# Input statistics handed over from the first stage, their normalisation moved to ScalarE, square roots in place of Newton steps, a transposed shared expert, and weights loaded behind the activations

## The chip, the cores and the metric

The kernel runs on one core of one Trainium2 chip. The metric is the device time of one execution in microseconds (us), the median of several. Before the change three runs gave 4096.03 us (4090.68 to 4097.14).

## What is computed

A small vision tower over 128 images. Tokenising gives 169 tokens of 128 values for each image; two layers follow, each of an attention and a feed-forward part, all with a residual and a layer norm in front. In short:

```
h = tok(x)                                    # 5 shifted contexts, norm, 8x8 patches -> (128, 169, 128)
h = h + neuron_attention(norm(h))             # 256 neurons, softmax(scale / (dist + 0.1))
h = h + fp8_linear(norm(h), weight)           # 128x128, scaled by the largest |norm(h)| of all tokens
h = h + softmax(n n^T / sqrt(512)) n          # n = norm(h), over the 169 tokens of an image
h = h + shared_experts(n) + routed(n)         # n = norm(h); 2 shared, 64 routed, 6 of them for a token
```

The routed part: a router gives logits (with a bias), the six best experts of each of the 21632 tokens get a gate, each expert takes at most 4056 tokens, and computes silu(n wg) * (n wu) times its down matrix.

## The kernel before

**Front stage** (`front`, some 850 us). All images' tokens stand in SBUF. It makes `h` up to the neuron attention (`h1`), in 43 groups of four token positions, keeps mean and variance of each token in `mv1`, from which it finds the largest normalised value, and stores `h1` to DRAM (`h1d`).

**Middle stage** (first part of `back`). Two chains are braided by `braid` in numbered steps. A 'b' part runs for a pair of images in each of 64 steps: the fp8 linear and the attention over tokens. An 'r' part runs for a group of 512 rows of the result, 43 groups, in two of every three steps: norm, router, shared experts, ranks. `place_of` says in which step a group comes, `LATE` how many steps behind the pairs the groups begin. A part's number in the list is its lag: at lag 1 it works for the pair or group of the step before. Steps therefore come in threes: one without 'r' work (here called P, pair only), and two with it, Q (the one after P) and R (the one after Q). The lists in each engine's block give the order of the parts on that engine, and an engine takes them strictly in that order.

In a step VectorE (DVE) runs: `ffn_out` (adds the fp8 product to `h1`, statistics of the sum), `stats_q` (statistics of the next pair's `h1`), `choose` (logits, best experts), `silu_gate`, `attn_out`, `place`, `roots` (reciprocals of the roots that ScalarE makes), `norm_x`, `quant` (normalise `h1` and round it to fp8 values), `silu_up`, `denominator` (its last instruction completes a row, L1569), `norm` (statistics of the group, `rsqrt` by three Newton steps, the normalised row) and `shared_out`. TensorE (PE) runs: `count`, `shared_up`, `turn_x`, `scores`, `turn_q`, `ffn`, `turn_h`, `shared_down`, `mix`, `turn_r`, `route`. ScalarE (ACT) runs: `tanh`, `roots`, `probs`, `copy_x`, `expo`, `copy_q`, `copy_h`, `copy_x4`.

GpSimd (POOL) writes the finished rows (token, gates and its number) to the expert row buffer `xed` in DRAM, one indirect DMA for 128 rows and one choice: 24 for a group, 1014 in all (L991). A memset on a one-column tile behind each (L996) paces them. `norm` of group g waits until the 24 of group g-4 have landed, since `xr` has four buffers.

**Expert stage** (second part of `back`). `tables_late` turns the counts into lists of row blocks. SyncE (SP) loads four blocks of 128 rows at a time into `xin` (`load_rows`, here the same memory as `xr`), PE, ACT and DVE compute the experts, and POOL writes each block's results to `ytk` by an indirect DMA (`spread`, L1003, 1080 of them). After the first eight loads SP writes 64 blocks of `xed` with a neutral row (L1093). Near the end `add_up` sums the six results of each token.

**At the head of `back`** SP loads all weights of the second layer (L1028 to L1032), then the first `h1` (L1018); DVE waits for all of it and halves `wdt` (L1391), and PE and ACT wait too.

What sets the steps' numbers:

```python
    LATE = 7
    CUT = place_of(GSTEPS[0][1], LATE) + 1
```

and the wait behind which the loads of rows stand:

```python
            sp.wait_ge(n["tab_ready"], 2)
            scattered_up_to(GR)
```

Of the kernel before, what the change touches and what calls it, by code (L numbers as in the profile page):

```python
# [127 lines left out]
def braid(eng, begin, end, late, parts, r_first, r_stop):  # L128
# [8 lines left out]
    def do(i, u):  # L137
        third, m = (u - late) % 3, (u - late) // 3
        c = 2 * m + (third == 2)
        for kind, lag, fn in parts:  # L140
            if kind == 'b':
                g = period * i + (u - lag)
                if not isinstance(g, int) or 0 <= g < nb + (lag == 0 and fn.__name__ == "roots"):
                    fn(g, (u - lag) % 2, 3 * i + (u - lag) // 2)
# [19 lines left out]
def build(nc, io):  # L164
# [11 lines left out]
    with ExitStack() as ctx:  # L176
# [3 lines left out]
        def sem(name):  # L180
# [14 lines left out]
        fscale = sb("fscale", [128, 4])  # L195

        front(nc, io, sb, bank, wide, dict(
            ident=ident, identb=identb, ones=ones, onesb=onesb, before=before, beforeb=beforeb,
            eps_ln=eps_ln, tenth=tenth, wq=wq, fscale=fscale), h1d, gbd, ytk)
        back(nc, io, sb, sem, bank, wide, dict(  # L200
            ident=ident, identb=identb, ones=ones, onesb=onesb, before=before, beforeb=beforeb,
            wq=wq, fscale=fscale, eps_ln=eps_ln), h1d, h3d, h4d, xed, ytk, out)


def front(nc, io, sb0, bank, wide, c, h1d, gbd, ytk):
# [7 lines left out]
    with ExitStack() as ctx:  # L213
        def sb(name, shape, dt=F32):
            return sb0(name, shape, dt, ctx)
# [56 lines left out]
        zeros = sb("zeros", [128, 768])  # L272
# [21 lines left out]
        with nc.Block() as block:  # L294
# [24 lines left out]
            def _(g):  # L319
# [7 lines left out]
                g.memset(zeros[:, :], 0.0).then_inc(s_zero, 1)  # L327
                g.wait_ge(s_const, 7)
# [156 lines left out]
        s_amall = sem("s_amall")  # L485

# [4 lines left out]
        with nc.Block() as block:  # L491
            @block.sync
            def _(sp):
# [19 lines left out]
                sp.wait_ge(s_zero, 1)  # L513
# [32 lines left out]
            def _(pe):  # L546
# [49 lines left out]
                pipeline(pe, 0, GA, [(2, turn), (4, turn_probs), (2, cross), (4, mix), (0, conv)])  # L596

# [58 lines left out]
            def _(v):  # L656
# [102 lines left out]
                link(v.reciprocal(hmin[:, :], hstd[:, :]))  # L759
                link(v.tensor_tensor(hmax[:, :], hmax[:, :], hmin[:, :], ALU.mult))  # L760
# [13 lines left out]


# [13 lines left out]
def rsqrt(v, var, eps, out, xe, half, done, base):  # L789

    v.tensor_scalar(xe, var, eps, None, ALU.add).then_inc(done, 1)
    v.wait_ge(done, base + 1)
    v.tensor_scalar(half.bitcast(I32), xe.bitcast(I32), 1, None, ALU.logical_shift_right).then_inc(done, 1)
    v.wait_ge(done, base + 2)
    v.tensor_scalar(out.bitcast(I32), half.bitcast(I32), -1.0, float(0x5F3759DF), ALU.mult, ALU.add).then_inc(done, 1)
    for k in range(3):
        v.wait_ge(done, base + 3 + 3 * k)  # L800
        v.tensor_tensor(half, out, out, ALU.mult).then_inc(done, 1)
        v.wait_ge(done, base + 4 + 3 * k)
# [1005 lines left out]
```

## Time and profile before

| | before |
|---|---|
| median of 3 runs | 4096.03 us (4090.68 to 4097.14) |
| the profiled execution, its own time | 4103.54 us |
| its span | 4101.7 us |
| mean granted TensorE clock | 0.678 |
| PE busy | 2888.1 us (70%) |
| DVE busy | 2655.3 us (65%) |
| ACT busy | 1512.4 us (37%) |
| POOL busy | 2720.8 us (66%) |

The span counts from the first to the last instruction. Busy shares are means over stages with different limits; the sections below read single stages. In the trace's rows a time in brackets is how long the engine had stood idle before the instruction, and the name behind the arrow what ended it. SPq is SyncE issuing a transfer.

### The profile page before, as it was taken

The numbers are of one execution on the slowest core, as the hardware profiler recorded it, in microseconds if no ns is written. First come the engines' busy times: TensorE is split into PE (matmuls) and PEld (weight loads), VectorE is DVE, ScalarE is ACT, GpSimd is POOL, SyncE is SP. The second block draws the span as 40 slices with busy tenths as digits, with TensorE's granted clock in tenths as the row PEclk, the third lists the DMA queues.
The fourth block names the chain that finished last, engine by engine and source line by source line (L and its number), as shares of the span: only waits on it lengthen the run. The fifth ranks groups of instructions, "written<-read, shape, count | busy, mean of one in ns | idle before, by whom it ended". The sixth has DMA issues, their size and how long they took to land. (4 is left out here: it accounts for less than half of the span.)

```text
span 4101.7 us, 75982 instructions
## 1 busy us (share of the span) xinstructions
PE 2888.1 (70%) x14869; PEld 2249.8 (55%) x14870; DVE 2655.3 (65%) x10164; ACT 1512.4 (37%) x3699; POOL 2720.8 (66%) x4427
## 2 busy tenths in 40 slices
PE   2988888727777777777767752687777777767770
PEld 2767777614544445454544531576676666666660
DVE  4588888846888888888778761344444444466664
ACT  2566666613232323323223211333433344333330
POOL 1355555400687777777757886588888888887881
PEclk7699999855555555555555556677878888877675
DMA  3555555321233333333323224544444444489867
GB/s 158 173 194 189 196 185 186 138 79 29 93 120 106 118 104 116 102 105 93 97 69 93 91 79 117 153 139 140 142 141 138 139 142 134 134 261 290 263 175 256
DMA packets 427082, 582.16 MB, mean 142 GB/s; under 512 B 64858, under 2 KB 345594, under 8 KB 415444
## 3 DMA queue, kind: packets, MB, share of 16 engines
q1 hardware_dynamic: 343668, 418.11, 33.7%
q0 software_dynamic: 83232, 162.29, 11.7%
q14 instruction: 149, 1.22, 0.1%
q8 instruction: 33, 0.54, 0.1%
HBM read 299.55 MB, written 306.56 MB: 148 GB/s over the span
## 5 line engine op out<-in xcount | busy, mean ns | idle before, releaser
L991 POOL DMA_INDIRECT xed<-xr,idxs x1014 | 1002.4, 989 | 528.0 <-POOL pace L996 188.9
L1003 POOL DMA_INDIRECT ytk<-yo,idxy x1080 | 1078.7, 999 | 297.5 <-POOL pace L1008 207.5
L1242 PE MATMUL wide<-wdt,hT 64*128 x2160 | 374.3, 323 | 360.4 <-DVE hT L1720 359.6
L1702 DVE TENSOR_TENSOR idxy<-xr 128x1 int32<-128x1 f32 x1080 | 148.2, 163 | 643.7 <-DMA ytk<-yo,idxy 640.9
L1242 PEld LDWEIGHTS wide<-wdt,hT 64*128 64x128 f32 x2160 | 314.3, 221 | 416.3 <-issue 413.7
L1378 ACT ACTIVATE yo<-wide,gd 128x128 f32<-128x128 f32 x1080 | 307.8, 368 | 633.7 <-PE wide L1242 615.9
L1224 PE MATMUL bank<-wgu,xeT 128*128 x2160 | 388.7, 340 | 0.0
L1224 PEld LDWEIGHTS bank<-wgu,xeT 128*128 128x128 f32 x2160 | 369.6, 258 | 1.5
L537 POOL TENSOR_TENSOR lnr<-rr,scb 128x1024 f32<-128x1024 f32 (+1 forms) x43 | 125.0, 2907 | 354.3 <-ACT rr L631 354.3
L1151 PE MATMUL wide<-xn,e 128*128 128x128 f32 (+3 forms) x1024 | 324.1, 449 | 0.0
L526 POOL TENSOR_TENSOR weff<-w,gam 128x640 f32<-128x640 f32 x169 | 260.7, 1571 | 86.3 <-POOLq L294 77.0
L1214 PE MATMUL bank<-ident,xr 128*128 128x128 f32 x1080 | 225.0, 347 | 100.8 <-DMA xr<-xed 100.8
L554 PE MATMUL bank<-weff,xs 128*128 128x128 f32 x1690 | 258.1, 306 | 14.7 <-DMA gbx<-gbd 14.7
L1151 PEld LDWEIGHTS wide<-xn,e 128*128 128x128 f32 (+3 forms) x1024 | 182.0, 234 | 124.4 <-issue 123.0
L554 PEld LDWEIGHTS bank<-weff,xs 128*128 128x128 f32 x1690 | 230.2, 214 | 32.8 <-DMA gbx<-gbd 15.7
L1363 ACT ACTIVATE xeT<-bank 128x512 f32<-128x512 f32 x270 | 163.2, 604 | 210.4 <-PE bank L1214 210.2
L1214 PEld LDWEIGHTS bank<-ident,xr 128*128 128x128 f32 x1080 | 179.1, 184 | 107.5 <-issue 101.3
L1140 PE MATMUL bank<-xnT 128*128 128x169 f32 (+1 forms) x512 | 202.3, 523 | 37.4 <-ACT xnT L1307 37.4
L1233 PE MATMUL wide<-ident,hh 128*64 128x128 f32 x1080 | 220.3, 341 | 0.0
L1130 PE MATMUL bank<-ident,xn 128*128 128x128 f32 (+1 forms) x256 | 87.5, 394 | 151.8 <-DVE xn L1451 151.8
L592 PE MATMUL bank<-v,eT 128*128 128x128 f32 x676 | 128.9, 369 | 82.9 <-issue 74.0
L1720 DVE COPY hT<-wide 64x512 f32<-64x512 f32 x270 | 182.1, 674 | 6.9 <-PE wide L1233 6.9
(312 smaller groups left out, 5918.6 us busy)
## 6 DMA issues: line engine op xcount, KB each, us to landing
xr<-xed SPq DMA_DIRECT2D x1080, 113.0 KB
ytk<-zeros SPq DMA_DIRECT2D x42, 1536.0 KB, 9.4
yg<-ytk SPq DMA_DIRECT2D x42, 1536.0 KB
xs<-in_xcol SPq DMA_DIRECT2D x42, 1280.0 KB
ytk<-yo,idxy POOLq DMA_INDIRECT x1080
xed<-xr,idxs POOLq DMA_INDIRECT x1014
H<-in_ximg SPq DMA_DIRECT2D x4, 2704.0 KB, 18.1
h1d<-H SPq DMA_DIRECT2D x42, 256.0 KB, 2.0
```

Source lines behind the costliest of these rows:

```text
L526: ins = p.tensor_tensor(weff[:, slot, j, :, :], w5[:, :, :], gam[:, bass.ds(TG * g + j, 1), :].rearrange("p o c -> p (o c)").unsqueeze(2). ...
L554: pe.matmul(dst, xs[:, slot, j, k, :], weff[:, slot, j, k, :], start=(k == 0), stop=False)
L991: p.indirect_dma_start(xed[:, :], bass.IndirectOffsetOnAxis(ap=idxs[:, slot, j, k:k + 1], axis=0), xr[:, slot, j, :], None, bounds_check=Z ...
L1003: p.indirect_dma_start(ytk[:, :], bass.IndirectOffsetOnAxis(ap=idxy[:, slot, j:j + 1], axis=0), yo[:, slot, j, :], None, bounds_check=128 ...
L1140: last = pe.matmul(dst, xnT[:, i, 128 * h:128 * h + m], xnT[:, i, 0:T], start=True, stop=True)
L1151: last = pe.matmul(pP[0:m, 256 * i + D * h:256 * i + D * h + D], e[0:m2, i, 128 * h:128 * h + m], xn[0:m2, slot, 2 * i + h2_, :], start=(h ...
L1214: last = pe.transpose(eT_[slot % 2][:, j * 128:(j + 1) * 128], xin[:, slot, j, 0:D], ident[:, :])
L1224: last = pe.matmul(eG[slot % 2][:, j * 128:(j + 1) * 128], xeT[:, slot % 2, j, :], wgu[:, bass.ds(e, 1), :].rearrange("p o f -> p (o f)"), ...
L1233: last = pe.transpose(eH[slot % 2][0:F, j * 128:(j + 1) * 128], hh[:, slot % 2, j, :], ident[:, :])
L1242: last = pe.matmul(eO[slot % 2][:, j * D:(j + 1) * D], hT[:, slot % 2, j, :], wdt[:, bass.ds(e, 1), :].rearrange("p o f -> p (o f)"), star ...
L1378: last = a.activation(yo[:, slot, j, :], eO[slot % 2][:, j * D:(j + 1) * D], ACT.Copy, scale=gd[:, slot, j:j + 1])
L1720: v.tensor_copy(hT[:, slot % 2, :, :].rearrange("p j d -> p (j d)"), eH[slot % 2][0:F, :])\
```

## The change

- The front stage transposes `mv1`'s means and reciprocal deviations on PE into a new table `mur` (scale and bias for each token of each pair, with the fp8 scale in it).
- `stats_q` is gone. ACT gets `norm_q` at the head of each step: a copy of eight values from `mur`, then four activations that write the scaled, normalised `xq`. `quant` on DVE keeps the clamp and the rounding.
- `roots` becomes `root_x` (root of the pair's variance, lag 1) and `root_r` (root of the group's, lag 0); `rsqrt` is gone. DVE takes the group's statistics at the head of the step (`stats_r`).
- The shared experts' gate and up products have the weights as the stationary operand and the 512 rows as the moving one: one product in place of four, with a transposed result. `turn_h` and `copy_h` are gone.
- The halves in `wdt` and `sdt` move into the gates and into `shared_out`.
- `LATE` is 6. The weights are loaded by ACT's queue, after the first two pairs' `h1`; nobody waits for them until `route`, and for the experts' until the expert stage.
- `xin` has memory of its own. The first row loads wait for the scatters of the first 30 groups only; those of all groups are waited for after block quad 164 (`Q0`).

```diff
-        zeros = sb("zeros", [128, 768])
+        zeros = sb("zeros", [128, 384])
...
+                pe.wait_ge(xT_ready, GA)
+                pe.wait_ge(s_rs1, 1)
+                for half, (t0, m) in enumerate(zip((0, HALF[0]), HALF)):
+                    pe.transpose(psT[0:m, half * 128:(half + 1) * 128], hmin[:, t0:t0 + m], ident[:, :])
+                    last = pe.transpose(psT[0:m, (2 + half) * 128:(3 + half) * 128], mv1[:, t0:t0 + m, 0], ident[:, :])
+                last.then_inc(s_mrT, 1)
...
-    LATE = 7
+    LATE = 6
...
-            sp.wait_ge(n["s_c"], 3)
-            sp.dma_start(wgu[:, :, :], io["wgu"]).then_inc(n["s_wt"], 16)
-            sp.dma_start(wdt[:, :, :], io["wdt"]).then_inc(n["s_wt"], 16)
...
+            sp.wait_ge(n["s_h1"], 1)
...
-            scattered_up_to(GR)
+            sp.wait_ge(n["s_zr"], 16)
+            scattered_up_to(C1)
             rows = [(0, load_rows)]
...
             sp.wait_ge(n["tail_z"], 16 * NE)
+            scattered_up_to(GR)
...
-                for j in range(nj):
-                    last = pe.matmul(rC[:, j * 128:(j + 1) * 128], x4T[:, j, :], sgu[:, 0:2 * F], start=True, stop=True)
-                last.then_inc(n["gate_done"], 1)
+                pe.matmul(rC[:, 0:nj * 128], sgu[:, 0:2 * F], x4T[:, 0:nj, :].rearrange("p j d -> p (j d)"),
+                          start=True, stop=True).then_inc(n["gate_done"], 1)
...
-            def turn_h(g, slot, rnd):
+            def shared_down(g, slot, rnd):
                 pe.wait_ge(n["hs_r"], g + 1)
                 for j in range(tiles_of(g)):
-                    last = pe.transpose(rA[:, j * 128:(j + 1) * 128], hs[:, j, :], ident[:, :])
-                last.then_inc(n["hst_done"], 1)
...
+                    last = pe.matmul(rA[:, j * D:(j + 1) * D], hs[:, j, :], sdt[:, :], start=True, stop=True)
                 last.then_inc(n["sh_done"], 1)
...
+            def norm_q(g, slot, rnd):
+
+                a.wait_ge(h1_in[slot], 32 * (rnd + 1))
+                a.activation(mrs[:, slot, :], mur[:, bass.ds(2 * g, 2), :, :].rearrange("p i h m -> p (i h m)"), ACT.Copy)\
+                    .then_inc(n["mrs_r"], 1)
+                a.wait_ge(n["mrs_r"], g + 1)
+                after(a, n["xqb_r"], g)
+                for j in range(4):
+                    last = a.activation(xq[:, j, :], h1s[:, slot, j, :], ACT.Identity, scale=mrs[:, slot, 2 * j:2 * j + 1],
+                                        bias=mrs[:, slot, 2 * j + 1:2 * j + 2])
+                last.then_inc(n["xq_r"], 1)
...
+            a.wait_ge(h1_in[0], 32)
+            a.wait_ge(h1_in[1], 32)
+            a.dma_start(rwt[:, :], io["rwt"]).then_inc(n["s_ws"], 16)
...
+            a.dma_start(wgu[:, :, :], io["wgu"]).then_inc(n["s_wt"], 16)
+            a.dma_start(wdt[:, :, :], io["wdt"]).then_inc(n["s_wt"], 16)
...
-                braid(a, *span, [('r', 1, halves(tanh)), ('b', 0, roots), ('r', 1, probs), ('b', 1, copy_x), ('b', 1, expo),
-                                 ('b', 0, copy_q), ('r', 1, halves(copy_h)), ('r', 0, halves(copy_x4))], s0, s1)
+                braid(a, *span, [('b', 0, norm_q), ('r', 1, halves(tanh)), ('b', 1, root_x), ('r', 0, root_r),
+                                 ('r', 1, probs), ('b', 1, copy_x), ('b', 1, expo),
+                                 ('b', 0, copy_q), ('r', 0, halves(copy_x4))], s0, s1)
...
-                braid(v, *SPAN[k], [('b', 1, ffn_out), ('b', 0, stats_q), ('r', 1, choose), ('r', 1, halves(silu_gate)),
-                                    ('b', 2, attn_out), ('r', 1, place), ('b', 0, roots), ('b', 1, norm_x),
-                                    ('b', 0, quant), ('r', 1, halves(silu_up)), ('r', 1, denominator), ('r', 0, norm),
-                                    ('r', 1, shared_out)], a, b)
+                braid(v, *SPAN[k], [('b', 1, ffn_out), ('r', 0, stats_r), ('r', 1, choose), ('r', 1, halves(silu_gate)),
+                                    ('b', 2, attn_out), ('r', 1, place), ('b', 1, root_x), ('r', 0, root_r),
+                                    ('b', 1, norm_x), ('b', 0, quant), ('r', 1, halves(silu_up)), ('r', 1, denominator),
+                                    ('r', 0, norm), ('r', 1, shared_out)], a, b)
```

How the order on the engines moves, at three places. First ACT's queue between a step R and the pair-only step P behind it, before (`x4T` is `copy_x4` of step R, `sd` the roots of step P):

```order
L1335 ACTIVATE x4T<-wide 128x512
L1324 REGISTER_ALU
L1327 ACT_TABLE_LOAD
L1327 ACTIVATE sd<-xe,eps_ln 128x8
L1307 ACTIVATE xnT<-bank 128x2x169
```

and now (line numbers of the changed kernel):

```order
L1343 ACTIVATE x4T<-wide 128x512
L1305 ISA
L1306 ISA
L1306 ACTIVATE mrs<-mur 128x8
L1308 REGISTER_ALU
L1311 ACTIVATE xq<-h1s,mrs 128x128 x4
L1319 ACT_TABLE_LOAD
L1319 ACTIVATE sdb<-mvc,eps_ln 128x4
L1289 ACTIVATE xnT<-bank 128x2x169
```

Five activations of `norm_q` have come between the copy and the root.

Second, DVE at the head of a step with 'r' work, from `ffn_out` to `choose`, before:

```order
L1442 SCALAR_TENSOR_TENSOR h<-bank,fscale,h1s 128x512
L1397 BN_STATS bstc<-h 128x6 x4
L1402 BN_AGGR mvc<-bstc 128x2 x4
L1446 TENSOR_SCALAR xe<-mvc 128x4
L1397 BN_STATS bstb<-h1s 128x6 x4
L1399 REGISTER_ALU
L1402 BN_AGGR mvb<-bstb 128x2 x4
L1409 TENSOR_SCALAR xe<-mvb 128x4
L1491 TENSOR_TENSOR lo<-wide,rbias 128x4x64
```

and now:

```order
L1430 SCALAR_TENSOR_TENSOR h<-bank,fscale,h1s 128x512
L1396 BN_STATS bstc<-h 128x6 x4
L1401 BN_AGGR mvc<-bstc 128x2 x4
L1396 BN_STATS bstd<-h3s 128x6 x4
L1398 REGISTER_ALU
L1401 BN_AGGR mvd<-bstd 128x2 x4
L1485 TENSOR_TENSOR lo<-wide,rbias 128x4x64
```

The statistics of the next pair have gone, those of the group have come from the step's end to their place.

Third, PE at the end of such a step, from `ffn` to `mix`, before:

```order
L1122 MATMUL bank<-wq,xqT 128x128 x4
L1201 MATMUL wide<-ident,hs 128x128 x4
L1207 MATMUL wide<-sdt,hsT 128x128 x4
L1145 REGISTER_ALU
L1151 MATMUL wide<-xn,e 128x128 x2
```

and now:

```order
L1111 MATMUL bank<-wq,xqT 128x128 x4
L1189 MATMUL wide<-sdt,hs 128x128 x4
L1140 MATMUL wide<-xn,e 128x128 x2
```

The transposition of `hs` has gone from between them.

## Rows read from the trace of the kernel before

**Rows 1.** Windows: length, busy PE, PEld, DVE, ACT, POOL; clock, DMA share, GB/s.

```profile
400.00:760.00 360.00, 321.30 (x1924) 256.69 (x1924) 307.29 (x847) 241.62 (x394) 201.56 (x110) 0.91 0.56 191
...
1500.00:2000.00 500.00, 376.06 (x1536) 249.71 (x1536) 401.60 (x1728) 154.38 (x439) 382.40 (x687) 0.50 0.33 104
```

**Rows 2.** Timeline of POOL in the middle stage: start, duration, instruction, [idle before].

```profile
1526.82 0.97 POOL L991 DMA_INDIRECT xed<-xr,idxs  x1 [6.32 <-DVE xr L1569]
...
1528.09 0.97 POOL L991 DMA_INDIRECT xed<-xr,idxs  x1 [0.19 <-POOL pace L996]
```

**Rows 3.** Timeline of POOL: first scatter, group 36's first, first spread, a gap, last spread.

```profile
1044.54 1.31 POOL L991 DMA_INDIRECT xed<-xr,idxs  x1 [183.03 <-issue]
...
2324.93 0.97 POOL L991 DMA_INDIRECT xed<-xr,idxs  x1 [2.71 <-issue]
...
2537.47 0.97 POOL L1003 DMA_INDIRECT ytk<-yo,idxy  x1 [18.25 <-ACT yo L1378]
...
2594.70 0.97 POOL L1003 DMA_INDIRECT ytk<-yo,idxy  x1 [31.27 <-issue]
...
4016.99 0.97 POOL L1003 DMA_INDIRECT ytk<-yo,idxy  x1 [0.19 <-POOL pace L1008]
```

**Rows 4.** Timeline of SP and DVE at the end of the lists and the start of the experts.

```profile
2460.56 0.21 DVE L1687 CAST ttail<-wide 1x64 int32<-1x64 f32 x1
...
2542.70 40.09 SPq L1093 DMA_DIRECT2D xed<-zrow  x64
```

**Rows 5.** Timeline at the head of the second part: POOL, SP, DVE.

```profile
852.40 0.95 POOL L973 MEMSET h1s<- 128x1024 f32 x1
...
866.25 17.75 SPq L1018 DMA_DIRECT2D h1s<-h1d  x1
...
885.69 4.42 DVE L1391 TENSOR_SCALAR wdt<-wdt 64x8192 f32<-64x8192 f32 x1 [34.92 <-DMA xed<-zrow]
...
896.20 0.49 DVE L1425 TENSOR_SCALAR xq<-xq,fscale 128x512 f32<-128x512 f32 x1
```

**Rows 6.** Timeline of DVE over three steps, P, Q and R: each `ffn_out`, and three instructions between.

```profile
1630.29 0.74 DVE L1442 SCALAR_TENSOR_TENSOR h<-bank,fscale,h1s 128x512 f32<-128x512 f32 x1
...
1637.21 1.24 DVE L1451 TENSOR_SCALAR xn<-h,mvc,root 128x128 f32<-128x128 f32 x4
...
1646.79 0.75 DVE L1442 SCALAR_TENSOR_TENSOR h<-bank,fscale,h1s 128x512 f32<-128x512 f32 x1 [4.43 <-PE bank L1122]
...
1672.04 0.74 DVE L1442 SCALAR_TENSOR_TENSOR h<-bank,fscale,h1s 128x512 f32<-128x512 f32 x1
...
1679.61 0.43 DVE L1491 TENSOR_TENSOR lo<-wide,rbias 128x256 f32<-128x256 f32 x1 [3.77 <-PE wide L1169]
...
1687.09 1.12 DVE L1451 TENSOR_SCALAR xn<-h,mvc,root 128x128 f32<-128x128 f32 x4
...
1701.13 0.74 DVE L1442 SCALAR_TENSOR_TENSOR h<-bank,fscale,h1s 128x512 f32<-128x512 f32 x1
```

**Rows 7.** Timeline of PE: `mix` of step P, then instructions of step R.

```profile
1628.74 4.91 PE L1151 MATMUL wide<-xn,e 128*128 128x128 f32 x15
...
1670.75 5.12 PE L1151 MATMUL wide<-xn,e 128*128 128x128 f32 x16
...
1695.34 0.61 PE L1122 MATMUL bank<-wq,xqT 128*128 128x128 bf16 x4 [1.29 <-ACT xqT L1301]
...
1695.74 1.06 PE L1201 MATMUL wide<-ident,hs 128*128 128x128 f32 x4
...
1697.49 2.08 PE L1207 MATMUL wide<-sdt,hsT 128*128 128x128 f32 x8 [0.69 <-ACT hsT L1357]
```

**Rows 8.** Timeline of ACT in step P: the last copy of step R, then the root.

```profile
1634.73 0.60 ACT L1335 ACTIVATE x4T<-wide 128x512 f32<-128x512 f32 x1 [8.12 <-PE wide L1159]
...
1636.64 0.30 ACT L1327 ACTIVATE sd<-xe,eps_ln 128x8 f32<-128x8 f32 x1
```

**Rows 9.** A group of instructions: busy us, mean ns of one, idle before.

```profile
L1378 ACT ACTIVATE yo<-wide,gd 128x128 f32<-128x128 f32 x1080 | 307.8, 368 | 633.7 <-PE wide L1242 615.9 <-issue 16.0 <-DVE gd L1697 1.8
```

More of the change, by code:

```diff
@@ L142, in do @@
                 g = period * i + (u - lag)
-                if not isinstance(g, int) or 0 <= g < nb + (lag == 0 and fn.__name__ == "roots"):
+                if not isinstance(g, int) or 0 <= g < nb:
                     fn(g, (u - lag) % 2, 3 * i + (u - lag) // 2)
@@ L786, in quantise @@
     link(v.tensor_tensor(dst, tmp, mag, ALU.subtract))
[L789 to L802, printed above, removed]
-        v.scalar_tensor_tensor(half, half, -0.5, xe, ALU.mult, ALU.mult).then_inc(done, 1)
-        v.wait_ge(done, base + 5 + 3 * k)
-        v.scalar_tensor_tensor(out, half, 1.5, out, ALU.add, ALU.mult).then_inc(done, 1)
-    v.wait_ge(done, base + RSQRT_STEPS)
-RSQRT_STEPS = 12
 def back(nc, io, sb0, sem, bank, wide, c, h1d, h3d, h4d, xed, ytk, out):
     ident, identb, ones, onesb = c["ident"], c["identb"], c["ones"], c["onesb"]
-    before, beforeb, wq, fscale = c["before"], c["beforeb"], c["wq"], c["fscale"]
+    before, beforeb, wq, fscale, mur = c["before"], c["beforeb"], c["wq"], c["fscale"], c["mur"]
     NB = B // 2
@@ L910, in back @@
     hs = sb_early("hs", [128, TG, 2 * F])
-    hsT = sb_early("hsT", [128, TG, D])
     early.close()
-    xin = xr
+    xin = sb("xin", [128, ES, TG, XW])
+    xink = xin[:, :, :, :].bitcast(BF16)
     xeT = sb("xeT", [128, 2, TG, 128])
@@ L1283, in stage @@
                 braid(pe, *span, [('r', 1, halves(count)), ('r', 1, halves(shared_up)), ('b', 1, turn_x),
-                                  ('b', 1, scores), ('b', 0, turn_q), ('b', 0, ffn), ('r', 1, halves(turn_h)),
-                                  ('r', 1, halves(shared_down)), ('b', 1, mix), ('r', 0, turn_r),
+                                  ('b', 1, scores), ('b', 0, turn_q), ('b', 0, ffn), ('r', 1, halves(shared_down)), ('b', 1, mix), ('r', 0, turn_r),
                                   ('r', 0, halves(route))], a, b)
@@ L1351, in probs @@
                 last.then_inc(n["ex_r"], 1)
-            def copy_h(g, slot, rnd):
-                nj = tiles_of(g)
-                a.wait_ge(n["hst_done"], g + 1)
-                after(a, n["sh_done"], g)
-                a.activation(hsT[:, 0:nj, :].rearrange("p j d -> p (j d)"), rA[:, 0:nj * 128], ACT.Copy)\
-                    .then_inc(n["hsT_r"], 1)
             def copy_xe(q, slot, rnd):
```

149 lines of the change are left out of this document (74 added, 75 removed).

## The prediction

> **What bounds the kernel now.** I read the windows first, then the timeline of one engine after another where the windows left it open, and last the timeline of the joints between the stages.
>
> The windows [rows 1] say that no engine is full in the middle stage: DVE is busy 402 of 500 us, POOL 382, PE 376, and TensorE's clock is granted at 0.50, the lower of its two levels, where the front stage has 0.91. So waits between engines set the pace, and each must be looked for.
>
> POOL's timeline shows a floor. Two scatters in a row start 1.27 us apart [rows 2], so a group's 24 cost 31 us. POOL does idle, 6.3 us in front of a group until DVE has completed its rows [rows 2]: today it waits for DVE. From group 36 on it no longer does: from there to the first spread's idle time, 2324.9 to 2519.2, lie 150 scatters at 1.295 us [rows 3]. So the middle stage is "first scatter, then 36 groups at the braid's pace, then some 194 us at POOL's".
>
> The expert stage is POOL's too: from 2594.7 to 4017.0 it issues about 1060 spreads, 1.34 us each [rows 3]. In front of it stand two holes: 18.25 us until the first result is there, and 31.27 us with nothing to spread [rows 3]. In the second SP issues 64 stores of neutral rows, 40.1 us [rows 4], and block loads stand behind them. The lists were done at 2460.8 [rows 4], 58 us before POOL ended its scatters; SP waited for these.
>
> The braid's pace needs three steps [rows 6]. P lasts 16.50 us (1630.29 to 1646.79), Q 25.25, R 29.09, together 70.8 for two groups, where POOL's floor is 61 to 63. DVE waits in P for the fp8 product (4.43) and in R for the router's logits (3.77). In Q it is full.
>
> **The change part by part.** Each term is a shift of the time at which POOL ends.
>
> *Start.* Today the first `quant` begins at 896.2, after weights (DVE idle 34.9), a scaling of 4.4 and the pair's statistics [rows 5]. Now POOL clears `h1s` first, at 852.4 plus 0.95. The first loads of `h1` need about 5 us to be issued and land; ACT then issues seven transfers, which at the 0.3 to 0.7 us that SP's took is 3.6 us, and runs `norm_q`. That gives a `quant` at 864. The front stage's end gains four transpositions and four small DVE instructions, about 2 us. I take -30 us. Bounds: -33, and -14 if ACT is held in its issues as SP was for 17.75 us behind nine transfers [rows 5]; ACT has seven of its own, so I stay near the first.
>
> The transfers that used to be waited for still move. SP's next `h1` load meets them. It is wanted a step, some 15 us, later, and today all weights are in 24 us after their issue. So it costs nothing, or at most 5 us if it comes in last.
>
> The Trainium skill (DMA: Bandwidth & Descriptors, "Issuing engines are not separate DMA queues") says that transfers started by different engines run on the same 16 DMA engines and interleave, so moving the weights to ACT frees no bandwidth. By that rule alone the start could lose those 5 us; the row cannot tell, as there one queue carried all.
>
> *One step less.* `LATE` 6 takes out a step with pair work only, which lasts about as P without its late root: -15 us. Its pair work comes back later, in POOL's 36 groups, where it is paid already.
>
> *The braid.* DVE loses per step four statistics, their sums, two small copies and four normalising instructions, and per group twelve small ones. Summed from the timeline that is 3 us a step and 2.7 a group, 14 us of 70.8. How much of it is on the path?
>
> Q. From `ffn_out` to `norm_x` nothing changes much: four statistics go and four come, two copies go, a reciprocal comes; 11.1 us. Then PE's chain counts, not DVE. In R, `ffn` begins 8.25 us after `norm_x` (1687.09, 1695.34), the next product of `hs` 0.40 behind it, and `shared_down` lasts 2.08 [rows 6, 7]. With 0.2 for the signal and 0.6 for `shared_out`, the next `ffn_out` comes 11.5 us after `norm_x`. DVE would be through after 8.6. So it gets a new wait of 2.9 us in front of `shared_out`, which today it reaches as the product is done. Q = 22.6, -2.6.
>
> R. The logits come 8.86 us after `mix` begins (1670.75, 1679.61) [rows 6, 7]. `mix` now begins 1.0 us ahead of `ffn_out` (1.29 today), so DVE, ready at 3.5, waits until 7.9. From there to `norm_x` it is 7.5 us, and 0.2 for the second reciprocal: 15.6. With 11.5 R = 27.1, -2.0.
>
> P. This one gets longer. ACT's `copy_x4` comes 5.99 us after `mix` begins (1628.74, 1634.73) [rows 7, 8], so at 5.0, and lasts 0.6. Today the root's table load and root follow at once and end 1.61 us after the copy (1636.94). Now `norm_q` stands between. Its nearest row is 128x128 on ACT at 368 ns [rows 9], from PSUM; back-to-back and from SBUF I take four at 0.32, 0.25 for the copy of eight values and 0.2 for its signal, 1.75 us; the bounds are 1.3 (0.25 each) and 3. So the root is there at 8.95, `norm_x` starts at 9.25 (6.92 today), and `ffn_out` follows 9.2 us later (9.58 today, when PE was late with the gate product). P = 18.45, +1.95.
>
> Sum 68.15 against 70.84: -2.7. Some tenths of jitter are in today's rows and not in mine, so I carry -2.4, over 18 cycles -43 us. Bounds: -75 (nothing of `norm_q` on the path) to +5. The single 512-column product instead of four of 128 columns I price at nothing: the stretch before `norm_x` covers it, and were it half a microsecond longer it would show in R alone.
>
> *The joint.* SP no longer waits for the last scatters. The lists are ready 58 us or more before POOL's end. The first eight quads take some 21 us and the 64 stores 40.1: both fit, or miss by 3 us which eight ready quads (41 us of spreading) cover. So -18.25, and of the second hole all but the few us that a quad's turn costs: -46 in all. Bounds: -50, and -15 if stores and scatters get in each other's way. Own memory for `xin` is what allows it.
>
> After the joint nothing changes: 1080 spreads, then 84 us for the last sums.
>
> The smaller source of the zeros (twice as many descriptors) lies in the front stage, DMA at 0.56 [rows 1]: 0, at most +5.
>
> Sum: -30 - 15 - 43 - 46 = -134. The profiled execution took 4103.5, so it would take 3969.5; it stands 7.5 us above the median of the runs, which gives 3962.
>
> **The rivals.**
>
> *A: POOL becomes the bound.* The chain through PE shrinks enough that groups follow every 31.3 us, 62.6 a cycle. What would do it is TensorE's clock, if it came up to what the front stage has [rows 1]: `mix` alone lasts 5.1 us and `shared_down` 2.1 at 0.50 [rows 7], and both lie on the chain. For it: PE's holes get fewer (`turn_h` and its copy go). Against: the 3 us hole before `turn_x` stays in Q and R, and P gains one. Price: 70.2 - 62.6 = 7.6 a cycle, -137 in place of -43: 3868.
> The Trainium skill (TensorE: Matmul & The Clock Gate, "Part 1: The HAM clock gate") says that the half clock is the default and sustained activity releases it; by that rule denser work here could lift it. The trace agrees as far as it goes: 0.91 where PE is busy 89% of the time, 0.50 where it is 75% [rows 1].
>
> *B: the braid gives nothing.* `norm_q` takes 3 us, or the loop's register work delays ACT in R as well; P grows by 3.2 and more, and the cycle stays at 70 to 72. Then -134 + 43 to + 75: 4005 to 4037.
>
> *C: the joint gives nothing*, because 7.4 MB of neutral rows and the scatters share the DMA: 4008.
>
> *D: slower.* `norm_q` heads ACT's queue in all 64 steps, and in Q and R the root behind it has slack: in R some 2.8 us, in Q more. Beyond that every microsecond counts twice a cycle. Start, step and joint give 91 us, or 5 a cycle; with the 2.4 it takes x + (x - 2.8) = 7.4, so x = 5.1: it decides from a `norm_q` of 6.9 us, 1.6 us for an activation, or from an `h1` that comes late to ACT. At 9 us it would be -91 + 18 x 9.3 = +76: 4172. Against it: the nearest activation takes 0.37 [rows 9], and SP loads `h1` a step ahead.
>
> **How the numbers follow.** Forecast 3962, chance 0.58, its own range 3925 to 4000. A 0.18, B 0.13, C 0.06, D 0.03, and 0.02 for no difference. The range 3862 to 4020 takes in A, C and the lower half of B, and leaves out B's upper half and D. A measurement can tell about 0.2%, 8 us, from no change. Faster by more: 0.95; within: 0.02; slower: 0.03.
>
> **What would show it.** In the changed kernel's trace: the first `ffn_out` near 872 and the first scatter near 1000; P at 18 to 19 us, longer than today, with DVE waiting for ACT's root; in Q and R DVE waiting 2 to 3 us for `shared_down`; POOL still idle ahead of every second group; the first spread right behind the last scatter and no hole after it. A is right if POOL idles no more from early on and the clock stands above 0.6; B if P lasts over 20 us; C if the holes are there. I am wrong at the root if DVE shows no wait for PE in Q.

## The result, and the profile after

The changed kernel takes 3959.1 us (median of four runs, 3950.2 to 3960.1) against 4096.6 for the kernel before on the same chip: a ratio of 0.966, 95% interval 0.964 to 0.968. The prediction said 3962, in a range of 3862 to 4020. The profiled execution took 3959.3 us, with a span of 3957.4 where the one before had 4101.7.

The windows answer to [rows 1]: length, busy PE, PEld, DVE, ACT, POOL, then clock, DMA share, GB/s.

```profile
400.00:760.00 360.00, 320.23 (x1918) 255.33 (x1916) 307.27 (x845) 241.08 (x394) 201.55 (x110) 0.91 0.58 192
1500.00:2000.00 500.00, 360.91 (x1326) 202.03 (x1327) 326.88 (x1305) 188.84 (x550) 401.97 (x713) 0.52 0.33 106
```

The front stage is as it was. In the middle DVE has fallen from 402 to 327 us of 500, ACT has risen from 154 to 189, and POOL, whose scatters end the stage, from 382 to 402.

POOL's timeline, for [rows 3]: the first scatter, group 36's first, the last scatter and the first spread behind it, the last spread.

```profile
998.94 1.31 POOL L986 DMA_INDIRECT xed<-xr,idxs  x1 [134.37 <-issue]
...
2234.17 0.97 POOL L986 DMA_INDIRECT xed<-xr,idxs  x1 [3.04 <-DVE xr L1563]
...
2427.86 0.97 POOL L986 DMA_INDIRECT xed<-xr,idxs  x1 [0.19 <-POOL pace L991]
...
2429.14 0.97 POOL L998 DMA_INDIRECT ytk<-yo,idxy  x1 [0.19 <-POOL pace L991]
...
3875.30 0.97 POOL L998 DMA_INDIRECT ytk<-yo,idxy  x1 [0.19 <-POOL pace L1003]
```

These five times cut the span into pieces that add up. I cut every profiled execution of the study in the same way. A piece is the time of its last row less the time of its first; "joint" is from the last scatter's start to the first spread's. The upper six are from chips on which the kernel before takes 4096 to 4098 us. The lower eight are from two others, called the slow chips below: e1, e3, e5 and e7 from one on which it takes 5176 us, e2, e4, e6 and e9 from one on which it takes 5180.

| kernel | first scatter at | scatters | joint | spreads | rest | span |
|---|---|---|---|---|---|---|
| before | 1044.5 | 1473.6 | 19.3 | 1479.5 | 84.7 | 4101.7 |
| after | 998.9 | 1428.9 | 1.3 | 1446.2 | 82.1 | 3957.4 |
| after again (r1) | 1000.2 | 1404.0 | 1.3 | 1445.5 | 81.3 | 3932.3 |
| shared expert back (r2) | 1000.2 | 1503.9 | 1.3 | 1450.1 | 85.6 | 4041.2 |
| roots first (r3) | 996.2 | 1370.6 | 1.3 | 1444.1 | 79.9 | 3892.1 |
| joint undone (r4) | 999.8 | 1425.3 | 19.7 | 1479.3 | 85.8 | 4009.9 |
| roots first (e1) | 998.8 | 1918.1 | 15.4 | 1896.7 | 88.9 | 4917.9 |
| joint undone (e2) | 999.6 | 1913.9 | 25.7 | 1895.9 | 85.5 | 4920.5 |
| shared expert back (e3) | 1002.0 | 2067.5 | 29.0 | 1891.8 | 86.4 | 5076.8 |
| `LATE` 7 (e4) | 1015.3 | 1920.2 | 7.6 | 1895.9 | 85.6 | 4924.7 |
| before + transposed product (e5) | 1043.2 | 1954.7 | 31.1 | 1893.7 | 82.0 | 5004.8 |
| weights first (e6) | 1019.3 | 1904.5 | 13.1 | 1896.1 | 84.8 | 4917.8 |
| four DVE operations added (e7) | 1003.8 | 1962.9 | 14.6 | 1897.8 | 83.7 | 4962.8 |
| `norm_q` doubled (e9) | 1001.8 | 1922.6 | 11.0 | 1896.1 | 84.9 | 4916.5 |

So the 144.3 us are 45.6 ahead of the first scatter, 44.7 in the scatters (45.2 of it ahead of group 36, from the second row here and in [rows 3]), 18.0 at the joint, 33.3 in the spreads (the second hole, 31.3 in [rows 3]) and 2.6 behind them.

Now the steps. DVE's timeline over P and Q and the start of R, with the rows that answer to [rows 6]; what stands in brackets is the idle time before and what ended it:

```profile
1631.16 0.74 DVE L1430 SCALAR_TENSOR_TENSOR h<-bank,fscale,h1s 128x512 f32<-128x512 f32 x1
...
1640.39 0.18 DVE L1408 RECIPROCAL rb<-sdb 128x4 f32<-128x4 f32 x1 [3.64 <-ACT sdb L1319]
1640.60 1.11 DVE L1438 TENSOR_SCALAR xn<-h,mvc,rb 128x128 f32<-128x128 f32 x4
...
1649.49 0.75 DVE L1430 SCALAR_TENSOR_TENSOR h<-bank,fscale,h1s 128x512 f32<-128x512 f32 x1 [5.01 <-PE bank L1111]
...
1671.51 0.69 DVE L1573 SCALAR_TENSOR_TENSOR h<-wide,h3s 128x512 f32<-128x512 f32 x1 [2.91 <-PE wide L1189]
1672.12 0.74 DVE L1430 SCALAR_TENSOR_TENSOR h<-bank,fscale,h1s 128x512 f32<-128x512 f32 x1
...
1698.48 0.69 DVE L1573 SCALAR_TENSOR_TENSOR h<-wide,h3s 128x512 f32<-128x512 f32 x1 [2.77 <-PE wide L1189]
1699.09 0.74 DVE L1430 SCALAR_TENSOR_TENSOR h<-bank,fscale,h1s 128x512 f32<-128x512 f32 x1
```

P lasts 18.33 us (1631.16 to 1649.49), Q 22.63, R 26.97: 67.9 where it was 70.8. DVE now stands 3.64 us for ACT's root in P, 5.01 for the fp8 product, and 2.91 and 2.77 for `shared_down` (L1189) in Q and R. ACT's timeline in P shows the late root, for [rows 8]:

```profile
1636.37 0.60 ACT L1343 ACTIVATE x4T<-wide 128x512 f32<-128x512 f32 x1 [8.46 <-PE wide L1148]
1636.86 0.20 ACT L1306 ACTIVATE mrs<-mur 128x8 f32 x1
1637.10 1.65 ACT L1311 ACTIVATE xq<-h1s,mrs 128x128 f32<-128x128 f32 x4
1638.77 1.28 ACT L1319 ACT_TABLE_LOAD   x1
1640.06 0.30 ACT L1319 ACTIVATE sdb<-mvc,eps_ln 128x4 f32<-128x4 f32 x1
```

The copy of eight values and the four activations of `norm_q` stand between `x4T` and the root's table load and take 1.9 us.

### The profile page after: what moved, and what is told of

The parts are those of the page before. It is cut to its first block and busy times, and to the rows that moved or that the text cites. A ratio compares the mean times of both kernels' runs of the same rounds, so it can differ in the third digit from the quotient of the medians.

```text
span 3957.4 us, 73441 instructions
## 1 busy us (share of the span) xinstructions
PE 2841.1 (72%) x14200; PEld 2118.6 (54%) x14201; DVE 2396.3 (61%) x8796; ACT 1620.1 (41%) x4026; POOL 2729.5 (69%) x4427
## 5 line engine op out<-in xcount | busy, mean ns | idle before, releaser
L1224 PE MATMUL wide<-wdt,hT 64*128 x2160 | 388.0, 332 | 392.4 <-DVE hT L1714 391.6
L1224 PEld LDWEIGHTS wide<-wdt,hT 64*128 64x128 f32 x2160 | 328.4, 230 | 449.7 <-issue 447.3
L1696 DVE TENSOR_TENSOR idxy<-xin 128x1 int32<-128x1 f32 x1080 | 147.8, 163 | 693.6 <-DMA ytk<-yo,idxy 692.4
L1140 PE MATMUL wide<-xn,e 128*128 128x128 f32 (+3 forms) x1024 | 307.2, 429 | 0.0
L559 PE MATMUL bank<-weff,xs 128*128 128x128 f32 x1690 | 258.7, 307 | 14.6 <-DMA gbx<-gbd 14.6
L1140 PEld LDWEIGHTS wide<-xn,e 128*128 128x128 f32 (+3 forms) x1024 | 174.0, 224 | 117.1 <-issue 112.4
L1196 PE MATMUL bank<-ident,xin 128*128 128x128 f32 x1080 | 224.4, 347 | 8.8 <-DMA xin<-xed 8.8
L1119 PEld LDWEIGHTS bank<-ident,xn 128*128 128x128 f32 (+1 forms) x256 | 45.7, 178 | 310.2 <-DVE xn L1438 251.5
L1196 PEld LDWEIGHTS bank<-ident,xin 128*128 128x128 f32 x1080 | 178.0, 183 | 15.3 <-issue 8.5
```

The lines of the kernel that those rows point to most:

```text
L559: pe.matmul(dst, xs[:, slot, j, k, :], weff[:, slot, j, k, :], start=(k == 0), stop=False)
L1140: last = pe.matmul(pP[0:m, 256 * i + D * h:256 * i + D * h + D], e[0:m2, i, 128 * h:128 * h + m], xn[0:m2, slot, 2 * i + h2_, :], start=(h ...
L1196: last = pe.transpose(eT_[slot % 2][:, j * 128:(j + 1) * 128], xin[:, slot, j, 0:D], ident[:, :])
L1224: last = pe.matmul(eO[slot % 2][:, j * D:(j + 1) * D], hT[:, slot % 2, j, :], wdt[:, bass.ds(e, 1), :].rearrange("p o f -> p (o f)"), star ...
```

## The experiments

Eight kernels ran on the slow chips: what the text on record says in absolute microseconds is meant for the first chip, and only differences between kernels on the same chip can be read. The changed kernel itself was never run there. The last four, with the changed kernel itself among them, ran together on a chip on which the kernel before took 4097.9 us.

### One part undone each, beside the changed kernel

**r1**, the changed kernel as it is.

> The changed kernel itself, unaltered, as the base for the three kernels beside it. On a chip like the first (before at 4096 us) it should take 3959 us, 0.966 of before. On a chip like the second (before at 5175 us) no run of it exists: the five kernels that differ from it by one small step took 4917 to 4930 us there, so it should take 4900 to 4930 us, about 0.951 of before. Should it be under 4880 us there, then each of those small steps costs on that chip what it was meant to cost; should it be at 4920 us, none of them reaches the time there.

3942.9 us (3934.2 to 3958.3), 0.9635 of before (0.9606 to 0.9663). It is 16 us below the first measurement, and its own runs lie 24 us apart. The table puts the difference of the profiled executions, 25 us, into the scatters alone; what varies there is told behind r3.

**r2**, the shared expert as it was.

```diff
-                pe.matmul(rC[:, 0:nj * 128], sgu[:, 0:2 * F], x4T[:, 0:nj, :].rearrange("p j d -> p (j d)"),
-                          start=True, stop=True).then_inc(n["gate_done"], 1)
+                for j in range(nj):
+                    last = pe.matmul(rC[:, j * 128:(j + 1) * 128], x4T[:, j, :], sgu[:, 0:2 * F], start=True, stop=True)
+                last.then_inc(n["gate_done"], 1)
...
-('r', 1, halves(shared_down)), ('b', 1, mix), ('r', 0, turn_r),
+('r', 1, halves(turn_h)), ('r', 1, halves(shared_down)), ('b', 1, mix), ('r', 0, turn_r),
```

> Shared expert as it was (four gate, four up matmuls, a transpose of h and its copy by ACT), the rest as changed. Theory (the braid's rounds are a chain of about 20 waits, and the two rounds with rest work lose the copy and the transposes): Q and R take 25 and 29 us again, 4.5 us a cycle over 18 cycles less what the clock gives back, so 45 us slower than the changed kernel on a chip like the first, 3995 to 4010 us. Rival (POOL bound, the steps only fill its idle time): under 10 us slower. On a chip like the second the distance to the changed kernel was not to be had; with it at 4920 us it would be 160 us, far over the theory's 45, and then something beside the braid's arithmetic (the missing instructions themselves) is worth more there.

4043.0 us (4042.6 to 4046.5): 100 us slower than r1 and 84 slower than the first measurement of the changed kernel, about twice the 45 expected. Nearly the whole difference stands in the scatters (1503.9 against 1404.0; against the first profile of the changed kernel 75). DVE's and ACT's timeline of r2 in a step Q and a step R:

```profile
1691.30 0.75 DVE L1447 SCALAR_TENSOR_TENSOR h<-bank,fscale,h1s 128x512 f32<-128x512 f32 x1 [5.00 <-PE bank L1112]
...
1714.98 0.69 DVE L1590 SCALAR_TENSOR_TENSOR h<-wide,h3s 128x512 f32<-128x512 f32 x1 [4.64 <-PE wide L1199]
1715.59 0.74 DVE L1447 SCALAR_TENSOR_TENSOR h<-bank,fscale,h1s 128x512 f32<-128x512 f32 x1
...
1743.68 0.69 DVE L1590 SCALAR_TENSOR_TENSOR h<-wide,h3s 128x512 f32<-128x512 f32 x1 [4.33 <-PE wide L1199]
1744.29 0.74 DVE L1447 SCALAR_TENSOR_TENSOR h<-bank,fscale,h1s 128x512 f32<-128x512 f32 x1
```

```profile
1712.12 0.60 ACT L1375 ACTIVATE hsT<-wide 128x512 f32<-128x512 f32 x1 [1.55 <-PE wide L1193]
```

Q is 24.3 and R 28.7. DVE's wait for `shared_down` is 4.64 and 4.33 us, 1.6 to 1.7 more than in the changed kernel: the transposes and the copy back to SBUF. The DVE work that the change took out hides none of it; it only shifts the wait. So at the lower clock the transposed product is worth 3.3 us a cycle, 60 us over 18, and all the rest of the change is worth 1.0 us in Q and 0.4 in R (25.25 and 29.09 before). I put the other 15 to 40 down to steps at the higher clock, which r2 hardly has; that is argued from the counts that follow, and not shown. Of the 14 steps P between the first groups and the one long step (from 1940 us in the changed kernel, 42.8 us), 13 last over 18 us in r2, 10 and 8 in the two profiles of the changed kernel. The mean cycle over that stretch (13 cycles, from one P's `ffn_out` to the next) is 71.2 us in r2, 67.2 and 66.1 in those two, 69.5 before.

**r3**, the roots ahead of `norm_q` in ACT's order.

```diff
-                braid(a, *span, [('b', 0, norm_q), ('r', 1, halves(tanh)), ('b', 1, root_x), ('r', 0, root_r),
+                braid(a, *span, [('r', 1, halves(tanh)), ('b', 1, root_x), ('r', 0, root_r), ('b', 0, norm_q),
```

> norm_q (four ACTIVATEs, 1.65 us, and a small one before them) put behind both roots in ACT's order. Theory (the root that DVE waits 3.6 us for in P comes that much earlier): P falls by 1.5 to 1.9 us, over 18 cycles 27 to 34 us, if what then waits for norm_q (the copy of q and DVE's quantizing) has room; 3925 to 3935 us on a chip like the first. Rival (the quantizing needs norm_q's result at the place where the root was needed, so the wait moves from the root to norm_q): the same time within 10 us, 3950 to 3965 us. On a chip like the second: no difference over 10 us to the changed kernel, since it took 4926 us there among 4917 to 4930 for the others.

3905.7 us (3894.0 to 3922.5), 0.9545 of before (0.9516 to 0.9575) and 37 us under r1. This version beats both kernels. DVE's timeline in a step P of it at the lower clock, then in one at the higher:

```profile
1723.52 0.74 DVE L1430 SCALAR_TENSOR_TENSOR h<-bank,fscale,h1s 128x512 f32<-128x512 f32 x1
...
1730.97 0.18 DVE L1408 RECIPROCAL rb<-sdb 128x4 f32<-128x4 f32 x1 [1.86 <-ACT sdb L1319]
...
1732.76 0.43 DVE L1414 TENSOR_SCALAR xq<-xq 128x512 f32<-128x512 f32 x1 [0.46 <-ACT xq L1311]
...
1740.62 0.75 DVE L1430 SCALAR_TENSOR_TENSOR h<-bank,fscale,h1s 128x512 f32<-128x512 f32 x1 [5.03 <-PE bank L1111]
```

```profile
1660.59 0.74 DVE L1430 SCALAR_TENSOR_TENSOR h<-bank,fscale,h1s 128x512 f32<-128x512 f32 x1
...
1673.08 0.75 DVE L1430 SCALAR_TENSOR_TENSOR h<-bank,fscale,h1s 128x512 f32<-128x512 f32 x1 [2.28 <-PE bank L1111]
```

The root comes 1.8 us earlier, `norm_q` behind it costs DVE 0.46 us ahead of the quantizing, and P is 17.1 in place of 18.3. Of the 1.9 us of `norm_q` all but some 0.7 was to be had in such a step. That makes 22 us over 18 cycles; the mean cycle fell by 2.6 us, from 66.1 to 63.5, and 2.1 of it is in P (a mean of 17.2 in r1, 15.1 in r3). The windows of these two steps (the same columns as above):

```profile
1724.00:1741.00 17.00, 14.40 (x48) 7.94 (x47) 7.21 (x26) 8.46 (x21) 14.28 (x26) 0.50 0.39 126
1661.00:1673.00 12.00, 8.31 (x47) 4.71 (x47) 7.10 (x25) 7.80 (x20) 10.00 (x18) 1.00 0.48 152
```

The same 47 or 48 products take 14.4 us at a clock of 0.50 and 8.3 at 1.00, and P is 4.6 us shorter. So a step at 2.4 GHz saves two and a half times the wait for the root (1.86). The order and the clock are not two separate gains, though. Here is a step P of each kernel in which the mean granted clock was 0.89 (1.00 for the first 10 us), in windows of its length, first r1 and then r3:

```profile
1160.70:1176.10 15.40, 10.10 (x48) 5.55 (x48) 7.71 (x26) 7.56 (x21) 13.28 (x25) 0.89 0.46 141
```

```profile
1217.30:1229.80 12.50, 8.90 (x49) 5.13 (x48) 7.53 (x26) 7.96 (x21) 10.99 (x19) 0.89 0.50 161
```

and what DVE waits for in them, in the same order:

```profile
1168.06 0.18 DVE L1408 RECIPROCAL rb<-sdb 128x4 f32<-128x4 f32 x1 [3.17 <-ACT sdb L1319]
...
1176.39 0.75 DVE L1430 SCALAR_TENSOR_TENSOR h<-bank,fscale,h1s 128x512 f32<-128x512 f32 x1 [4.20 <-PE bank L1111]
```

```profile
1222.50 0.18 DVE L1408 RECIPROCAL rb<-sdb 128x4 f32<-128x4 f32 x1 [1.40 <-ACT sdb L1319]
...
1229.91 0.75 DVE L1430 SCALAR_TENSOR_TENSOR h<-bank,fscale,h1s 128x512 f32<-128x512 f32 x1 [2.71 <-PE bank L1111]
```

P is 15.4 us in r1 and 12.5 in r3, 2.9 apart where it was 1.2 at 0.50: both waits are shorter. No step P of r1 in this stretch is under 15.4 us.

And r3 is close to POOL's floor. From group 6 to group 36 POOL stands 18.5 us for rows of DVE, all of it at the one long step; in r1 it stands 59.8 there, in the first profile of the changed kernel 88.4 and before 138.2. The window from 1200 to 2000 us, for r1, r2 and r3:

```profile
1200.00:2000.00 800.00, 565.85 (x2195) 317.17 (x2194) 536.12 (x2140) 312.80 (x908) 643.20 (x1148) 0.56 0.34 110
```

```profile
1200.00:2000.00 800.00, 588.02 (x2425) 390.68 (x2426) 507.12 (x2037) 303.08 (x874) 595.38 (x1071) 0.51 0.32 103
```

```profile
1200.00:2000.00 800.00, 568.76 (x2274) 321.15 (x2274) 564.54 (x2246) 326.04 (x948) 657.37 (x1167) 0.57 0.35 112
```

The clock is at 0.56, 0.51 and 0.57, and the first profile of the changed kernel has 0.53, below r1's. The Trainium skill (TensorE: Matmul & The Clock Gate, "Part 1: The HAM clock gate") has the full clock come with sustained activity. These rows neither bear that out nor speak against it: PE is busiest in r2, where the clock is lowest, but a product at the lower clock also counts as busy for longer. What decides for one step P and against the next stays open.

**r4**, the joint as before, `xin` keeping its own memory.

```diff
-            scattered_up_to(C1)
+            scattered_up_to(GR)
...
             sp.wait_ge(n["tail_z"], 16 * NE)
-            scattered_up_to(GR)
```

> The spreads' own buffer kept, but the expert stage waits for the last scatter before its first expert's rows as before. Theory (the start of the expert stage behind the last scatter is on the path): the hole ahead of the first spread comes back, 18 us, and the hole of 31 us behind the first ones stays filled or comes back in part; 10 to 30 us slower on a chip like the first, 3970 to 3990 us. Rival (the expert stage's end is set by POOL's 1080 spreads and the DMA, with slack): under 5 us. On a chip like the second 24 us of hole stood ahead of the first spread in this kernel and 14 us in the one with the roots first, and their times were 4925 and 4926 us, so no difference there.

4008.8 us (4008.2 to 4011.7), 66 us over r1 and 50 over the first measurement of the changed kernel. POOL's timeline of r4 at the joint:

```profile
2425.13 0.98 POOL L986 DMA_INDIRECT xed<-xr,idxs  x1 [0.19 <-POOL pace L991]
...
2444.82 0.97 POOL L998 DMA_INDIRECT ytk<-yo,idxy  x1 [18.60 <-ACT yo L1378]
...
2500.34 0.97 POOL L998 DMA_INDIRECT ytk<-yo,idxy  x1 [29.56 <-issue]
```

Both holes are back, at nearly the size of before (18.25 and 31.27, [rows 3]). In the table the joint is 18.4 us longer and the spreads 33.8: 52 us, the wait's whole price. My expectation was wrong in the second hole, which I thought would stay filled in part. The rest of the 66 are the scatters, 21 us longer than r1's but 4 shorter than in the first profile of the changed kernel; this edit doesn't touch them, and they are not its work.

### On the slow chips

Four kernels ran on one of them, beside the kernel before at 5175.5 us: the roots first, the shared expert back, the kernel before with nothing but the transposed product, and the changed kernel with four more DVE operations of 512 columns ahead of `shared_out`.

> The changed kernel with norm_q behind the two roots in ScalarE's queue instead of ahead of them. Theory (norm_q delays the root in the pair-only step P, and nothing else): P falls from 18.4 to about 16.6 us, Q and R stay at 22.6 and 27.0, so 1.8 us a cycle over 18 cycles: about 32 us less than the changed kernel, some 3927. Rival (P is held by the chain through TensorE, not by the root): no difference, 3959. Rival (norm_q now comes too late for quant): P stays or grows, 3959 or more.

> The changed kernel with the shared experts as before (four products with the rows stationary, turn_h and copy_h back). Theory (in Q and R the end of the step is set by TensorE's chain ffn, shared_down, shared_out, and VectorE waits 2.9 us there): the transposition and its copy, 1.75 us, come back on the path in Q and in R, 3.5 us a cycle, 63 us in all: some 4022. Rival (VectorE is the bound): at most the part above its 2.9 us of slack, so 0, 3959.

> The kernel before with the transposed shared experts alone. Theory: step Q is full of VectorE work and stays at 25.2, but mix starts 1.75 us earlier, so in R the logits and in P the copy ahead of the root come earlier: R 27.3 (from 29.1), P 14.9 (from 16.5), 3.3 us a cycle, about 60 us less than before: 4036. Rival (VectorE is the bound before, and this edit takes nothing from it): 4096.

```diff
+                for k in range(4):
+                    after(v, n["junk_r"], 4 * g + k)
+                    v.tensor_scalar(junk[:, 0:nj, :], h3s[:, slot, 0:nj, :], 1.0, None, ALU.mult).then_inc(n["junk_r"], 1)
```

> The changed kernel with four extra 512-column instructions on VectorE ahead of shared_out in each group (about 1.8 us, results unused). Theory: they fall into the 2.9 us that VectorE waits there: Q and R unchanged, within 5 us of 3959. Rival (VectorE sets the pace after the change): 3.6 us a cycle, 65 us more: 4024.

Measured, in this order: 4926.0, 5080.1, 5004.8 and 4962.7 us, ratios 0.952, 0.981, 0.967 and 0.958 to before (each to within 0.004). The transposed product alone (e5) takes 171 us off there, 3.3%, where 60 were expected; the kernel without it (e3) takes 154 more than e1, nearly all in the scatters, where 63 were expected. From e5 to e1, which adds everything else of the change (the roots first among it), the scatters lose 37 us. e3 and e7 have `norm_q` first and e1 has the roots first, so each distance to e1 holds that difference too. The four added operations, 2.0 us for each of the 43 groups, come with 45 us more in the scatters than in e1. DVE's wait ahead of `shared_out` falls from a mean of 2.47 us in e1 to 0.73, so 1.7 of the 2.0 go into it, as expected; most of the 45 us is not accounted for by that, and its cause stays open.

Four more ran on the other, beside the kernel before at 5180.2 us: joint undone (e2, as r4), the weights loaded first by SP and waited for by ACT and DVE, `LATE` 7, and `norm_q` with its four activations twice (the second set goes to a buffer that nobody reads).

> The changed kernel with the first row loads waiting for all scatters again. Theory: the two holes on GpSimd come back, 18 us ahead of the first spread and about 27 to 33 us behind the first quads: 46 to 51 us more than the changed kernel, 4005 to 4010. Rival (the holes' time is lost elsewhere, in transfers that meet the scatters): less than 20 us more.

> The changed kernel with the weights loaded by SyncE ahead of h1 and every engine waiting for them, as before (the scaling of wdt stays away). Theory: the first ffn_out moves from 872 to about 896, 24 us more, 3983, the rest unchanged. Rival (the weights behind the activations disturb the first steps as much as they save): less than 8 us more.

> The changed kernel with LATE = 7. Theory: one more step with pair work only before the first group, 15 us more, 3974; the groups' pace is unchanged. Rival (the end of the stage is set by the pairs, whose 64 steps are the same): 3959.

> The changed kernel with norm_q's four activations done twice (the first four into an unused tile), 1.65 us more on ScalarE at the head of each step. Theory: P grows by 1.65 us to 20.0, R has 2.8 us of slack and Q more, so both stay: 30 us more, 3989. Rival (norm_q is on the path in all three): 5 us a cycle, 89 us more, 4048. Rival (it is on no path): 3959.

```diff
+                after(a, n["junk_r"], g)
+                for j in range(4):
+                    last = a.activation(junk[:, j, :], h1s[:, slot, j, :], ACT.Identity, scale=mrs[:, slot, 2 * j:2 * j + 1],
+                                        bias=mrs[:, slot, 2 * j + 1:2 * j + 2])
+                last.then_inc(n["junk_r"], 1)
```

Measured 4924.8, 4930.2, 4916.8 and 4920.6 us, all within 14 us of each other; the ratios' intervals overlap. So none of the expected differences (46 to 51, 24, 15 and 30 us) shows in the whole time there. e1, from the other slow chip, is at 4926.0 among them: the order of the roots shows nothing there either. The local rows do show what each edit did. Weights first puts the first `ffn_out` at 895.3 in place of 871 to 873, and the first scatter 18 to 20 us later. `LATE` 7 puts the first scatter 14 to 16 us later. The doubled `norm_q` leaves the scatters within 9 us of e1 and e2, where r3 and r1 differ by 33 on the other chip: doubling it costs nothing to be seen where other waits are this long. Of the joint e2 shows 13 to 18 us more hole than the other three of its chip, and as much time for the spreads.

Why are these chips slow? POOL's timeline of e1 in the middle of the expert stage (pace settings left out), against the even 1.27 us of [rows 2]:

```profile
3505.23 0.97 POOL L998 DMA_INDIRECT ytk<-yo,idxy  x1 [0.19 <-issue]
...
3506.51 0.97 POOL L998 DMA_INDIRECT ytk<-yo,idxy  x1 [0.19 <-issue]
...
3511.49 0.97 POOL L998 DMA_INDIRECT ytk<-yo,idxy  x1 [3.90 <-issue]
```

and ACT's and PE's in the middle stage, where the logits' product is 7 us late:

```profile
1591.30 0.60 ACT L1343 ACTIVATE x4T<-wide 128x512 f32<-128x512 f32 x1 [13.14 <-remote]
```

```profile
1591.95 1.97 PE L1159 MATMUL wide<-rwt,x4T 128*128 128x64 f32 x8 [7.18 <-issue]
```

Everything up to the first scatter takes as long as on the other chips, to within 3 us for the same kernel. From there on both stages with scatters or spreads take 1.31 to 1.40 times as long (spreads 1896.7 against 1444.1, scatters 1918.1 against 1370.6, e1 and r3), and engines stand for releasers that the trace doesn't name. The slowness comes in the stages in which these indirect transfers run beside the rest. Whether the transfers themselves land later, or the instructions of the other engines are fetched later beside them, I have not separated: that stays open, and so does why the transposed product is worth 150 us there.

## Why the prediction was right

- **Start**, -30: the first `ffn_out` moved from 901.07 to 872.01, -29.1. e6 confirms the reason: with the weights in front again it is 24 us later. The loss of up to 5 us for transfers that meet on the way came too, one step later. The third pair's `h1`, which SP issued at 872.79, was not there for ACT until 889.45:

```profile
889.45 0.21 ACT L1306 ACTIVATE mrs<-mur 128x8 f32<-128x8 f32 x1 [6.53 <-DMA h1s<-h1d]
```

From 870 to 892 us the queue of the weights moved 4.28 MB and took 71% of the DMA engines' time. `norm_q` waited and the root behind it too, and that step lasts 18.4 us at a clock of 0.50. In r3, where the root doesn't stand behind `norm_q`, the same step lasts 15.4 at the same clock, so the late `h1` costs 3 us here, by the order on ACT. In e6, where the weights are there before, nothing waits for it, and of e6's 24 us 18 to 20 are left at the first scatter.
- **One step less**, -15: of the 45.6 us ahead of the first scatter 16.5 are left for the step and for all that changed in the steps ahead of the first scatter, the 3 us above among it; e4 gives 14 to 16 in the other direction. That these two terms reach the end of the kernel on the first chip is read from the pieces of the table and was not tried by a run: e4 and e6 ran on a slow chip alone, and there the first scatter moved and the whole time did not.
- **The braid**, -43: the scatters' stretch gives 44.7. P, Q and R at a clock of 0.50 are 18.3, 22.6 and 27.0 against a forecast of 18.45, 22.6 and 27.1, with the waits where they were to be. `norm_q` takes 1.9 us from the copy's start to its last activation; I had 1.75. In a sentence of its own: the Trainium skill (ScalarE: Activation LUTs, "What ACT_TABLE_LOAD costs") gives 280 ns + 0.833 ns per column for an activation with one pointer operand, 93 ns for a second and 93 ns of overlap, which for four of 128 columns is an estimate of 1.64 us, and the row has 1.65.
- But the -43 was a net sum of larger terms: -4.6 us a cycle for Q and R, some -83, and +1.95 for P. Of the first, 3.3 us a cycle are the shared expert's transposition at the lower clock, and it is worth -75 to -100 in the scatters (r2). What `norm_q` puts in front of the root costs +33 (r1 to r3). All of the change but the transposition comes to +30 (from before to r2: the mean cycle goes from 69.5 to 71.2 there, although DVE has less to do); so in this order of ACT's list only the transposition paid. My text priced P's growth at 1.95 us a cycle, 35 us (1.83 measured), and listed it as a term, without asking whether the order of two entries in ACT's list could take it back. It could, for nothing.
- **The joint**, -46: the holes gave 18.0 and 33.3, 51 together, and r4 brings 52 back. I had left some 3.5 us for a quad's turn, and nothing of the second hole is left: the spreads lost 33.3 us where it was 31.3.
- **After the joint**, 0: -2.6 in the last sums. The smaller source of zeros cost nothing to be seen.

In sum -144.3 in the span against -134; the 10 us too few are the joint's 5, the braid's 2 and the tail's 3. That the predicted time is within 3 us of the median all the same is luck: the profiled execution of before stood 7.5 us over its runs' median and that of after at it, and r1, the same kernel again, is another 16 us lower.

**The rivals.** A, POOL as the bound, is half there: POOL's groups of scatters start 31 to 32 and 33 to 37 us apart in turn, with 31 as the floor, and the clock went up only for single steps (0.52 from 1500 to 2000, not 0.9). In r3 A is there, but not by the clock, which is 0.57: outside the long step groups follow at 31.1 to 34.2. Its stretch of 1370.6 us stands against some 1320 for 42 groups at 31.4, and of these 50 us POOL stands only 22 for DVE: another 19 between groups 6 and 36 have no releaser in the profile. A faster braid has little left to give there. B fell, as P stayed under 20 us; so did C, as the holes are gone. Of D, r3 shows the sign of its mechanism (what stands ahead of the root is paid once a cycle), at 1.9 us and not at 6.9.

What the prediction did not have: at the turn of the loop over six steps, so in every other cycle, DVE stands ahead of `ffn_out` for nothing that the profile names (four times, from 1339 to 1743 us; the kernel before has no such wait). R takes it back in its slack for the logits, so that Q and R are 25.4 and 24.7 in place of 22.6 and 27.0. DVE's timeline of the changed kernel:

```profile
1606.42 0.75 DVE L1430 SCALAR_TENSOR_TENSOR h<-bank,fscale,h1s 128x512 f32<-128x512 f32 x1 [2.48 <-issue]
```

## What to carry to other kernels

A net term that comes out right can hide parts that are larger than it: write them down apart, and ask of each one with the wrong sign whether an order would remove it. Here a new piece of work with slack stood ahead of a root without any, and moving one entry of a list gave 33 us in the scatters beside the 45 of the whole braid and brought POOL close to its floor. And a gain measured on one chip is not the gain on the next: the transposed product was worth 2 to 2.5% on one and 3.3% on another, the joint 1.3 to 1.6% and nothing to be seen.

## What the runs showed of the hardware

- Of three chips of the same type the kernel before took 4098 us on one and 5176 and 5180 on the two others. The stages ahead of the first scatter were equal to within 3 us; those with scatters and spreads took 1.40 and 1.31 times as long (e1 against r3), and the last sums 89 us in place of 80.
- A table load on ACT lasts 1.28 us, and the root behind it starts 0.01 us after it ends (the rows of ACT above). The Trainium skill (ScalarE: Activation LUTs, "What ACT_TABLE_LOAD costs") adds a drain of some 1.38 us to every switch. The row speaks against it: the load starts 0.02 us after the activations ahead of it end, so neither side of it has room, and the measured 1.3 us for the switch is what I go by.
- Within one stage TensorE's clock changes from step to step, between 0.50 and 1.00, and the same step P lasts 17.1 us at 0.50 and 12.4 to 12.5 at 0.89 or 1.00 (r3). The four runs of r1 and r3 lie 24 and 28 us apart, those of r2 and r4 only 4; I take the clock for the reason, which is not shown: there are profiles of one execution each.
